# The attention's input also loaded features first and normalised there by POOL, with its row statistics sent through DRAM, in place of PE transposes

## What is computed

```python
h = jnp.maximum(_layernorm(x, axis=-1), 0.0)
x = x + _L0_gnn_ref(h, adj, adj, Wq, Wk, Wv, Wo)      # 16 heads of 32 features
h = jnp.maximum(_layernorm(x, axis=-1), 0.0)
x = x + _L1_gnn_ref(h, adj, router_w, router_b, expert_w, bn_gamma, bn_beta)

# L0: q, k, v = h @ Wq.T, h @ Wk.T, h @ Wv.T
a = jnp.einsum('bhnd,bhmd->bhnm', q, k) * scale + bias    # bias = adj + adj
p = jax.nn.softmax(a, axis=-1)
o = jnp.einsum('bhnm,bhmd->bhnd', p, v)                   # then o @ Wo.T
```

## Time and profile before

| | us |
|---|---|
| median of the runs (lowest, highest) | 1500.34 (1497.13, 1500.99) |
| profiled execution, its own time | 1500.94 |
| its span, first to last instruction | 1499.1 |
| PE busy | 1422.5 (95%) |
| DVE, ACT, POOL busy | 1146.7 (76%), 1010.8 (67%), 445.7 (30%) |
| mean granted TensorE clock | 0.981 of full |

### The profile page before, as it was taken

How to read it: one execution, slowest core, us unless ns; L and a number is a source line. 1 busy time by engine, 2 the same in 40 slices (tenths; PEclk the granted TensorE clock), 3 DMA queues, 4 the chain that set the end, 5 groups by cost and what they waited for, 6 DMA issues and landing times. The chain is left out here.

```text
span 1499.1 us, 38702 instructions
## 1 busy us (share of the span) xinstructions
PE 1422.5 (95%) x11218; PEld 1262.8 (84%) x11219; DVE 1146.7 (76%) x2704; ACT 1010.8 (67%) x3145; POOL 445.7 (30%) x529
## 2 busy tenths in 40 slices
PE   7999999999999999999999999999859999999885
PEld 6898989999999999999898999889748777777764
DVE  4787877778787877878777878777767777777684
ACT  4677777777777777777677777777645555554595
POOL 0222333332223233222322332222223444444100
PEclk9999999999999999999999999999879999999998
DMA  5965555666655666665556666664523432220898
GB/s 185 262 153 143 136 129 142 154 159 160 153 136 129 144 153 160 157 155 136 129 129 144 156 164 149 156 136 117 144 89 122 139 119 85 70 87 19 319 406 315
DMA packets 142137, 230.36 MB, mean 154 GB/s; under 512 B 17668, under 2 KB 34052, under 8 KB 142084
## 3 DMA queue, kind: packets, MB, share of 16 engines
q1 hardware_dynamic: 133636, 212.95, 54.6%
q10 hardware_dynamic: 8448, 16.78, 2.9%
HBM read 89.15 MB, written 39.85 MB: 86 GB/s over the span
## 5 line engine op out<-in xcount | busy, mean ns | idle before, releaser
L269 POOL TENSOR_TENSOR prob<-prob,norm 128x512 f32<-128x512 f32 x256 | 266.3, 1040 | 746.6 <-DVE norm L373 746.6
L302 ACT ACTIVATE prob<-logits,neg_max 128x128 f32<-128x128 f32 x1024 | 398.2, 393 | 86.3 <-DVE neg_max L362 86.3
L43 PE MATMUL bank<-hT_hi,w_hi 128*128 128x256 f32 x1024 | 302.8, 296 | 9.4 <-ACT v L326 7.0
L43 PE MATMUL bank<-hT_hi,w_lo 128*128 128x256 f32 x1024 | 292.1, 285 | 0.0
L43 PE MATMUL bank<-hT_lo,w_hi 128*128 128x256 f32 x1024 | 291.6, 285 | 0.0
L357 DVE SCALAR_TENSOR_TENSOR logits<-scores_ps,adj 128x512 f32<-128x512 f32 x256 | 176.7, 690 | 104.7 <-PE scores_ps L421 101.0
L309 ACT ACTIVATE probT<-probT_ps 128x512 f32<-128x512 f32 x256 | 152.7, 596 | 100.4 <-PE probT_ps L428 96.0
L43 PEld LDWEIGHTS bank<-hT_hi,w_hi 128*128 128x128 f32 x1024 | 198.3, 194 | 18.9 <-ACT v L326 10.2
L43 PEld LDWEIGHTS bank<-hT_lo,w_hi 128*128 128x128 f32 x1024 | 198.4, 194 | 0.0
L43 PEld LDWEIGHTS bank<-hT_hi,w_lo 128*128 128x128 f32 x1024 | 197.8, 193 | 0.0
L302 ACT ACTIVATION_READ_ACCUMULATOR prob<-logits,neg_max 128x1 f32 x1024 | 194.4, 190 | 0.0
(11 more groups left out here) (136 smaller groups left out, 2828.9 us busy)
## 6 DMA issues: line engine op xcount, KB each, us to landing
stack<-qk SPq DMA_DIRECT2D x768, 128.0 KB, 2.5
x_in<-in_x SPq DMA_DIRECT2D x32, 512.0 KB, 4.8
x_res<-in_x SPq DMA_DIRECT2D x64, 256.0 KB, 2.9
x_dram<-x_res SPq DMA_DIRECT2D x64, 256.0 KB, 2.6
x_in<-x_dram SPq DMA_DIRECT2D x32, 512.0 KB, 3.7
y<-outs ACTq DMA_DIRECT2D x16, 1024.0 KB, 11.8
w_hi<-x_dram SPq DMA_DIRECT2D x8, 1024.0 KB, 18.5
out_dram<-outs SPq DMA_DIRECT2D x24, 256.0 KB, 2.1
```

Source lines behind the costliest of these rows:

```text
L43: last = nc.tensor.matmul(out, a, b, start=(n == 0), stop=(n == len(terms) - 1))
L269: nc.gpsimd.tensor_tensor(prob[:, slot], prob[:, slot], norm[:, slot].unsqueeze(2).to_broadcast([N, R, N]), ALU.mult).then_inc(normed, 1)
L302: last = nc.scalar.activation(prob[:, slot, r], logits[:, slot, r], ACT.Exp, bias=neg_max[:, slot, r:r + 1], accum_out=row_sum[:, slot, r: ...
```

## The change

The input is given to the kernel twice, as x and as x_t, in which each pair of graphs lies features first. x_t goes by DMA (token T of SP) into xT, which takes the place of h. PE's H and ACT's A are gone. The statistics are still taken by DVE from x with a row per partition, now from one graph at a time (X0 and X1 load them into a single x_in). POOL's G makes rstd alone; -mean and rstd lie in stat. SP's new token B writes stat to stat_dram, 4 bytes to an element, waits until that has landed, and loads it back as a row that is given to all 128 partitions. POOL's new token U then adds -mean and multiplies by rstd, in place in xT, two operations of 128 x 512 for each graph. ACT's H rectifies xT into hT_hi, and DVE's H makes hT_lo from xT. The buffer adj_in is gone: J0 and J1' load one graph's adjacency each straight into adj2, once the logits of the pair before have been made from it, and D doubles it in place. Some tokens change place: N0 on DVE stands before B0, M in slot 2 and no longer in slot 4, G before P3. The warming transposes before the first turn are 120 and no longer 40.

```diff
-    x_in, h = x1_in[:, 0:2], x1_in[:, 2:4]
+    x_in = x1_in[:, 0]
+    row = x1_in[:, 1].rearrange("p (s g n) -> p s g n", s=2, g=2)
+    xT = x1_in[:, 2:4].rearrange("p g (a n) -> p (g a) n", n=N).rearrange("p (k g) n -> p k g n", g=2)
-    adj_in = sb("adj_in", [N, 2, N])
+    stat = sb("stat", [N, 2, 2])
+    neg_mean, rstd = stat[:, 0], stat[:, 1]
...
-    PE_ORDER = """S0 T6' H1' O0'
+    PE_ORDER = """S0 T6' O0'
                   S1 T7' Q0
...
                   S6 T4 W0 W1 W2 W3 V0
-                  S7 T5 H0 V1"""
+                  S7 T5 V1"""
...
-                   C4 A0 O0 E6
-                   A1 V0 C5 H0 E7"""
...
-    DVE_ORDER = """R7' L0 H1' B0
-                   N0 R0 L1 X0' B1
-                   N1 L2 R1 Q0 O1' B2
...
+                   C4 O0 E6
+                   V0 C5 H0 E7"""
+
+    DVE_ORDER = """R7' L0 H1' N0 B0
+                   R0 L1 X0' B1
+                   N1 L2 R1 M Q0 O1' B2
-                   M R3 L4 Q2 B4
+                   R3 L4 Q2 B4
...
-    POOL_ORDER = "P7' D1' P0 P1 P2 P3 G P4 D0 P5 P6"
-
-    SP_ORDER = "X K1' J Z1' Y0' Z0 K0 Y1'"
-    AHEAD = {"sp": dict(X=2, J=1, K=1), "pe": dict(Q=1, V=1, H=2), "act": dict(Q=1, V=1, H=2, A=2),
-             "dve": dict(Q=1, H=2, N=2, M=2), "pool": dict(G=2, D=1)}
-
-    START = {("act", -2): "U0 A0 A1 H0", ("act", -1): "H1' U1 U2 Q0 Q1 U3 Q2 Q3 A0 A1 V0 H0",
-             ("dve", -2): "N0 N1 M U0 H0", ("dve", -1): "H1' U1 U2 N0 N1 Q0 Q1 U3 M Q2 Q3 H0",
-             ("sp", 0): "X K1' J Z1' Y0' Z0 W K0 Y1'",
-
-             ("sp", PAIRS - 1): "K1' F Z1' Y0' Z0 Y1'",
+    POOL_ORDER = "P7' D1' P0 P1 P2 G P3 P4 U0 D0 P5 U1 P6"
+
+    SP_ORDER = "X1 K1' J1' T Z1' Y0' Z0 B J0 K0 Y1' X0"
+    AHEAD = {"sp": dict(X1=2, X0=3, T=2, B=2, J=1, K=1), "pe": dict(Q=1, V=1), "act": dict(Q=1, V=1, H=2),
+             "dve": dict(Q=1, H=2, N=2, M=2), "pool": dict(G=2, U=2, D=1)}
+
+    START = {("act", -2): "U0 H0", ("act", -1): "H1' U1 U2 Q0 Q1 Q2 Q3 U3 V0 H0",
+             ("dve", -2): "N0 N1 M U0 H0", ("dve", -1): "H1' U1 U2 N0 N1 M Q0 Q1 Q2 Q3 U3 H0",
+             ("sp", -2): "X0 B",
+             ("sp", -1): "X1 X0 T J0 B K0",
+             ("sp", 0): "X1 K1' J1' T Z1' Y0' Z0 W B J0 K0 Y1' X0",
+
+             ("sp", PAIRS - 1): "K1' J1' F Z1' Y0' Z0 Y1'",
...
+            load_x_res(0, 0)
+            load_x_res(0, 1)
+            load_xT(0)
+            load_w(0)
...
-                        sp.dma_start(x_in[:], x[bass.ds(2 * j, 2)].rearrange("g n f -> n g f")).then_inc(x_loaded, 16)
+                        if not isinstance(j, int) or (j, g) > (1, 0):
+                        sp.dma_start(x_in[:], x[bass.ds(2 * j + g, 1)].rearrange("g n f -> n (g f)")).then_inc(x_loaded, 16)
+                    elif token == "T" and not (isinstance(j, int) and j == 0):
+                        wait(sp, hT_split, 2 * j)
+                        load_xT(j)
+                    elif token == "B":
+                        wait(sp, rstd_ready, j + 1)
+                        with nc.allow_non_contiguous_dma(reason="two statistics of each row become rows"):
+                            sp.dma_start(stat_dram.rearrange("s g n -> n s g"), stat[:]).then_inc(stat_stored, 16)
+                        if isinstance(j, int) and j == 0:
+                            load_w(1)
+                            load_w(2)
+                        wait(sp, stat_stored, 16 * (j + 1))
+                        sp.dma_start(row[:], stat_dram.rearrange("(o s) g n -> o s g n", o=1).to_broadcast([128, 2, 2, N])).then_inc(row_loaded, 16)
+                        if isinstance(j, int) and j == 0:
+                            sp.wait_ge(w_split, 1)
+                            load_w(3)
                     elif token == "J":
-                        wait(sp, adj_doubled, 2 * j)
-                        sp.dma_start(adj_in[:], adj[bass.ds(2 * j, 2)].rearrange("g n m -> n g m")).then_inc(adj_loaded, 16)
-                    elif token == "Z":
+                        wait(sp, logits_ready, STEPS * (j - 1) + C * (g + 1))
+                        sp.dma_start(adj2[:, g], adj[bass.ds(2 * j + g, 1)].rearrange("g n m -> n (g m)")).then_inc(adj_loaded[g], 16)
...
-                        wait(pool, h_ready, 2 * j)
+                        wait(pool, stat_stored, 16 * j)
                         nc.gpsimd.tensor_tensor(rstd[:], var_eps[:], minus_half[:], ALU.pow).then_inc(rstd_ready, 1)
-                        wait(pool, rstd_ready, j + 1)
-                        nc.gpsimd.tensor_tensor(shift[:], neg_mean[:], rstd[:], ALU.mult).then_inc(shift_ready, 1)
+                    elif token == "U":
+                        wait(pool, xT_loaded, 16 * (j + 1))
+                        wait(pool, row_loaded, 16 * (j + 1))
+                        nc.gpsimd.tensor_tensor(xT[:, :, k], xT[:, :, k], row[:, 0, k].unsqueeze(1).to_broadcast([128, KC, N]),
+                                                ALU.add).then_inc(centred, 1)
+                        wait(pool, centred, 2 * j + k + 1)
+                        nc.gpsimd.tensor_tensor(xT[:, :, k], xT[:, :, k], row[:, 1, k].unsqueeze(1).to_broadcast([128, KC, N]),
+                                                ALU.mult).then_inc(scaled, 1)
                     elif token == "D":
-                        wait(pool, adj_loaded, 16 * (j + 1))
-                        wait(pool, logits_ready, STEPS * (j - 1) + C * (k + 1))
-                        nc.gpsimd.tensor_tensor(adj2[:, k], adj_in[:, k], adj_in[:, k], ALU.add).then_inc(adj_doubled, 1)
+                        wait(pool, adj_loaded[k], 16 * (j + 1))
+                        nc.gpsimd.tensor_tensor(adj2[:, k], adj2[:, k], adj2[:, k], ALU.add).then_inc(adj_doubled, 1)
...
-                    elif token == "A":
-                        wait(act, shift_ready, j + 1)
-                        wait(act, h_transposed, 2 * (j - 1) + k + 1)
-                        nc.scalar.activation(h[:, k], x_in[:, k], ACT.Relu, bias=shift[:, k:k + 1],
-                                             scale=rstd[:, k:k + 1]).then_inc(h_ready, 1)
                     elif token == "H":
-                        wait(act, h_transposed, 2 * j + k + 1)
-                        nc.scalar.activation(hT_hi[:, :, k], bank[:, H_BANK[k]].rearrange("p (c n) -> p c n", n=N),
-                                             ACT.Copy).then_inc(hT_hi_ready, 1)
+                        wait(act, scaled, 2 * j + k + 1)
+                        wait(act, v_projected, 2 * (j - 1) + k + 1)
+                        nc.scalar.activation(hT_hi[:, :, k], xT[:, :, k], ACT.Relu).then_inc(hT_hi_ready, 1)
...
-                        wait(dve, shift_ready, j)
+                        wait(dve, stat_stored, 16 * j)
...
-                        nc.vector.tensor_tensor(hT_lo[:, :, k], bank[:, H_BANK[k]].rearrange("p (c n) -> p c n", n=N),
-                                                hT_hi[:, :, k], ALU.subtract).then_inc(hT_split, 1)
+                        nc.vector.scalar_tensor_tensor(out=hT_lo[:, :, k], in0=xT[:, :, k], scalar=0.0, in1=hT_hi[:, :, k],
+                                                       op0=ALU.max, op1=ALU.subtract).then_inc(hT_split, 1)
...
-                        if exists(j + 2):
-                            wait(pe, *((hT_split, 2 * (j + 2) + 1), (qk_split, 4 * (j + 2) + 2))[k])
+                        if k == 1 and exists(j + 2):
+                            wait(pe, qk_split, 4 * (j + 2) + 2)
                         else:
                             wait(pe, x1_ready, 2 * j + k)
...
-                        wait(pe, *((hT_split, 2 * (j + 1)), (x1_ready, 2 * (j - 2) + 1), (v_copied, 2 * j),
+                        if k == 0:
+                            wait(pe, hT_split, 2 * (j + 1))
+                        wait(pe, *((v_copied, 2 * (j - 1) + 1), (x1_ready, 2 * (j - 2) + 1), (v_copied, 2 * j),
...
-                    elif token == "H":
-                        wait(pe, h_ready, 2 * j + k + 1)
-
-                        wait(pe, *((x1_ready, 2 * (j - 2)), (v_copied, 2 * (j - 1) + 1))[k])
-                        for kc in range(KC):
-                            last = nc.tensor.transpose(bank[:, H_BANK[k], 128 * kc:128 * kc + 128],
-                                                       h[:, k, 128 * kc:128 * kc + 128], ident[:])
-                        last.then_inc(h_transposed, 1)
-
-            keep_clock_up(nc, pe, bank[:, 0, 0:128], ident, 40)
+
+            keep_clock_up(nc, pe, bank[:, 0, 0:128], ident, 120)
```

More of the change, by code:

```diff
@@ L65, in scaled_moments, with attention_layer @@
     return nc.vector.tensor_scalar(m2[:], m2[:], 1.0 / count, EPS, ALU.mult, ALU.add)
-def attention_layer(nc, ctx, sem, ident, x, adj, weights, x1_dram, expert_w, shared):
+def attention_layer(nc, ctx, sem, ident, x, x_t, adj, weights, x1_dram, stat_dram, expert_w, shared):
     w_hi, w_raw, w_raw_loaded, ew_hi_ready, ew_split, x1_in, x1_loaded = shared
@@ L208, in run @@
             body(i)
-        with engine.Fori(2, PAIRS - 2) as i:
```

(37 more changed lines are left out.)

23 lines of the change are left out of this document (10 added, 13 removed).

## The result

The changed kernel takes 1964.4 us (median of four runs, 1962.0 to 1968.8) against 1498.7 (1495.9 to 1501.0) of the kernel before in the same comparison: 1.312 times as long, 95% interval 1.308 to 1.315. The direction was forecast; the time, 1815 us, was not, and it lies outside the range of 1735 to 1880.

The account below looks back on a forecast made before the run. The prediction took PE, full in the attention layer, as the bound, with a new wait before T0 deciding. It summed 1500.9 + 293 (turns 1 to 29) + 7 + 6 + 9 = 1816, forecasting 1815 us, range 1735 to 1880.

Parts of the forecast that it names:

- What bounds the kernel, the transposes: Attention turn: PE is full at 32.69 us; removing two graphs' transposes saves 0.90 us, giving 31.79 us without waits.
- The new wait, which decides: Before T0: POOL's D1' waits for J1' behind N0, X1 and K1', so PE stands still 9.3 us each turn.
- The trip through DRAM: Statistics row before U0: store and reload land at about T0 + 11.7 us, hidden with a store of 2.5 to 6 us.
- Rival B: SP's queue: a store over 8 us delays K0 and S0, adding 45 to 60 us, 1870 us in all; chance 0.10.
- The clock: PE after the wait before T0: half clock loses 1.7 us a turn, with 0 and 2.4 as the ends.
- Start and end: Outside turns 1 to 29: 9 us at the start, 7 in turn 0, 3 each in turns 30 and 31.
- Rival A: Before P0: D1' doesn't hold POOL, so the transposes' 28.8 us less the start's 9 give 1481 us; chance 0.06.

Follow-up runs that it names:

- e9: The change with 16-byte store, both graphs in x_in, separate row memory, D1' behind G, k/v weights behind the first row, X between J0 and K0: 1486.5 us.
- e11: e9 with turn 0's expert weights back ahead of the store of the statistics, as in the change: 1480.3 us, 0.988 times the kernel before.
- e2: The changed kernel with stat_dram laid out as 128 pieces of 16 bytes, the row read with a stride in U: 1771.3 us.
- e1: The changed kernel with J1' moved to the head of SP's turn, ahead of X1 and K1': 1771.5 us.
- e8: The change, 4-byte store kept, with both graphs in x_in, separate row memory, D1' behind G, X last on SP, k/v weights behind the first row: 1727.0 us.
- e4: The changed kernel with 64 useless transposes on PE in the wait before T0 of each turn: 1904.5 us.
- e3: The changed kernel with both edits of e1 and e2: 1654.9 us, 1.106 times the kernel before.
- e12: e9 with turn 0's expert weights moved behind K0: 1486.1 us, 0.992 times the kernel before.

## Why the prediction was wrong

**What bounds the kernel, the transposes:** right. PE full, 0.45 us per graph, 31.79 us a turn: e9 and e11 have just this turn. The 32.69 us that the prediction took for every turn of before is its commonest; the mean of its 31 turns is 33.0.

**The new wait, which decides:** right in its mechanism and in its links, up to the issue of J1' at 12.1 us. Mis-sized was the landing, 2.2 us for the 3.3 taken, which made the forecast 1.1 us a turn too long. With the store mended (e2) the change is the prediction's own case, with this wait alone: a turn of 41.5 us against 42.75, and 1771 us, within the range. e1 shows the link to J1': moved to the head of the queue, the wait is gone.

**The trip through DRAM:** this step failed. I wrote "I take 2.5 to 6 us, and up to there it is hidden"; it was 9.1 for the store and, where I had taken 2.9 from x_res, 5.4 in the median for the row. The row lay there 22 us after T0, not 11.7: the store went out at T0 + 7.5 (6.2 forecast), 9.1 and 5.6 us followed, and the step's own limit was T0 + 15.0. I had written of such a store that no row shows one, and then added up DMAs of 128 and 256 KB in long pieces; a row with many small pieces doesn't exist in that trace. e2 shows 193 us for it in the change, e8 135 in another order.

**Rival B** named this store, at a chance of 0.10, and put its price at K0 and S0, 45 to 60 us. Its condition came true at 9.1 us, but in the turns the price came by another way: not SP's queue, but POOL's. U0 stands ahead of P5, and T5 waits. In the turns K0 still landed in time; only at the start did it come late (below). A price of 5.94 us a turn, 172 in all, was three times that of the rival; I had costed what is queued behind the wait on SP, and not what is queued behind it on POOL.

**The clock:** right in kind, counted once where it comes twice. The single term of 1.7 us was 2.1 (e4), and the second wait, of only 2.99 us, was followed by 6.00 us at the half clock, another 2.95 lost. The Trainium skill (TensorE: Matmul & The Clock Gate, HAM oscillation) has the clock fall and rise again in each round of a loop with waits; the trace agrees, with two such falls a turn (a mean clock of 0.64 behind the first wait and of 0.50 behind the second), and e4 takes one away.

**Start and end:** 9 us forecast for the start, 27.9 measured, in two parts. The first projection came 17.8 us later than before (31.77 for 14.01), where 9 had been forecast: the store took 10.8 us there (issued at 8.04, the row at 18.80), with two weights of 1 MB issued right behind it, and the row 5.8. PE, idle for 14.3 us before that projection, ran from there to 40 us at a mean clock of 0.68. The other part the prediction left out: a second trip through DRAM stands ahead of the first K0.

```profile
42.75 0.38 SPq L255 DMA_DIRECT2D stat_dram<-stat  x1
54.87 0.33 SPq L260 DMA_DIRECT2D x_in<-stat_dram  x1
55.23 7.80 SPq L278 DMA_DIRECT2D stack<-qk  x12
```

This store took 12.1 us, and PE waited 13.1 us for the stacks before its first scores, 3.3 in the kernel before. It is the one place where rival B's own way, through K0, is seen. At the end of the layer 6 us had been forecast for turns 30 and 31, and turn 30 has 0.6; turn 0 has 16.5 where 7 had been forecast.

**What was not seen at all** is that X1's wait for N0 also delays ACT's Q0, through K1'. It cost nothing in the change, as it was hidden by the larger wait, but whoever had mended only the two known waits would have been 11% slower than before (e3).

Rival A, no stall at all, gave 1481 us; e11, in which its condition is made true by order and buffers, measures 1480.3. That they agree to a microsecond is partly luck. In e11 the first scores come 13.0 us late and not 9, and its first turn takes 38.63 us for 31.21 before. Against that its next 30 turns take 35.8 us less, of which 27 are the transposes; the rest is what the turns of before have above 32.69. ACT at times waits for the stacks there; that this is why they are longer is not shown. So a part of what e9 to e12 gain may come from the new place of X and not from the transposes; the kernel before with X moved was not run.

## What to carry to other kernels

A small transfer can't be priced by its bytes: the same 2 KB took 9.1 or 1.4 us by how they were cut into pieces. Count the elements that don't lie together, and if no row shows such a one, take the range as open above and look for who is queued behind its waiter on every engine. When a chain through a queue gets longer, list all consumers of each link, since the largest wait hides the others until it is mended. And a bulk load in an in-order queue belongs where the next transfer behind it isn't needed soon: moving one of 512 KB ahead of two tokens in the order was worth 106 us, and all that the change could give was 29.
